# Base gathers split five and three, first pair's loads on one queue, and a third PSUM set, in a two-layer kernel

## The reference, cut to what matters

```python
c   = einsum('bsi,boi->bso', x, weight[ids])            # layer 0, adapter of the sequence
lg  = c @ W_router.T                                    # 8 experts, top 2, softmax weights w
h   = einsum('td,erd->ter', c, lora_A)
x   = x + c @ W_base.T + b_base + 2 * einsum('ter,eor,te->to', h, lora_B, w)
y   = einsum('bct,bcd->bdt', x, weights[ids])           # layer 1, over the tokens
t   = y[:, perm] in 16 heads of 64
x   = x + unpermute(gelu(t @ up) @ down)
```

## Time and profile before

| | |
|---|---|
| median of 3 runs | 623.73 us (622.9 to 623.86) |
| the profiled execution | 626.12 us |
| its span, first to last instruction | 623.7 us |
| mean granted TensorE clock | 0.991 |
| HBM read, written | 98.09 MB, 8.39 MB |

### The profile page before, as it was taken

How to read it: one execution, slowest core, us unless ns; L and a number is a source line. 1 busy time by engine, 2 the same in 40 slices (tenths; PEclk the granted TensorE clock), 3 DMA queues, 4 the chain that set the end, 5 groups by cost and what they waited for, 6 DMA issues and landing times.

```text
span 623.7 us, 13533 instructions
## 1 busy us (share of the span) xinstructions
PE 601.5 (96%) x4439; PEld 349.5 (56%) x4440; DVE 440.6 (71%) x1233; ACT 139.7 (22%) x269; POOL 127.6 (20%) x194
## 2 busy tenths in 40 slices
PE   3899999999999999999899999999999999999996
PEld 2434444444444444447667676767676767676762
DVE  3026666666666666698787997879987889887862
ACT  0310000000000000054313432314341325232333
POOL 5000000111111110042012231313131313131313
PEclk9699999999999999999999999999999999999999
DMA  8978898898999989212022222222232323222222
GB/s 272 410 265 295 293 306 288 306 302 297 311 378 404 401 296 304 71 34 62 10 60 69 92 69 87 75 80 83 66 96 64 95 62 96 64 87 67 85 60 93
DMA packets 43425, 106.89 MB, mean 171 GB/s; under 512 B 8450, under 2 KB 17666, under 8 KB 43394
## 3 DMA queue, kind: packets, MB, share of 16 engines
q1 hardware_dynamic: 30914, 76.04, 35.4%
q0 software_dynamic: 6784, 21.51, 10.4%
q10 hardware_dynamic: 5696, 8.95, 4.3%
HBM read 98.09 MB, written 8.39 MB: 171 GB/s over the span
## 4 chain that ended last, share of the span: by engine, by line
PE 92%; DVE 3%; DMA 2%; issue 1%; DVEq 0%; ACT 0%; POOL 0%; ACTq 0%; SPq 0%; POOLq 0%
PE wide L494 33%; PE bank L596 18%; PE bank L604 9%; PE bank L676 8%; PE wide L659 8%; PE y_wide L525 4%; PE wide L509 3%; PE y_wide L639 2%; DMA x_in<-x_seq_dram 2%; PE bank L617 1%; PE bank L616 1%; PE bank L620 1%; DVE c_lo L1122 1%; PE wide L474 0%; PE bank L533 0%
## 5 line engine op out<-in xcount | busy, mean ns | idle before, releaser
L494 PE MATMUL wide<-ring,x_in 128*64 128x512 f32 x960 | 208.8, 592 | 0.0
L1171 DVE STREAM_TRANSPOSE x_tok<-xres 32x128 f32<-32x128 f32 x480 | 145.1, 302 | 6.3
L1013 DVE STREAM_TRANSPOSE c_pair<-wide 32x256 f32<-32x256 f32 x240 | 107.1, 446 | 56.9 <-issue 30.1
L494 PEld LDWEIGHTS wide<-ring,x_in 128*64 128x64 f32 x960 | 68.5, 137 | 128.6 <-issue 128.6
L866 ACT ACTIVATE act_sb<-wide 128x512 f32<-128x512 f32 x120 | 66.5, 610 | 192.9 <-PE wide L659 192.9
L596 PE MATMUL bank<-c_hi,base_t 128*128 128x512 f32 x384 | 102.3, 390 | 0.0
L393 POOL DMA_INDIRECT xres<-xT_dram,row_in x32 | 35.3, 1104 | 233.1 <-DVE out_sb L1162 229.8
L596 PEld LDWEIGHTS bank<-c_hi,base_t 128*128 128x128 f32 x384 | 71.9, 188 | 15.4
L604 PE MATMUL bank<-c_lo,base_t 128*128 (+1 forms) x256 | 78.3, 391 | 0.4 <-DVE c_lo L1122 0.4
L428 POOL COPY c_all<-c_pair 128x512 f32 x30 | 19.3, 670 | 222.8 <-DVE c_pair L1013 222.8
L676 PE MATMUL bank<-act_sb,down_sb 64*64 64x512 f32 x224 | 54.3, 602 | 0.0
(11 more groups left out here) (151 smaller groups left out, 578.0 us busy)
## 6 DMA issues: line engine op xcount, KB each, us to landing
ring<-adapters_dram SPq DMA_DIRECT2D x128, 512.0 KB, 5.8
x_in<-x_seq_dram ACTq DMA_DIRECT2D x32, 256.0 KB, 4.6
up_raw<-up_dram SPq DMA_DIRECT2D x64, 64.0 KB, 2.3
down_sb<-down_dram SPq DMA_DIRECT2D x32, 128.0 KB, 2.4
ar_sb<-lora_a_router_dram ACTq DMA_DIRECT2D x1, 544.0 KB, 4.3
mix_sb<-mix_dram SPq DMA_DIRECT2D x32, 16.0 KB, 2.0
xres<-xT_dram,row_in POOLq DMA_INDIRECT x32, 3.5
out_dram<-out_sb,row_out POOLq DMA_INDIRECT x28, 2.9
```

The source lines that it names most:

```text
L494: last = pe.matmul(acc[half][h][z * TOK:(z + 1) * TOK, :], x_in[:, half, z, k, :], ring[:, k, z, h * HALF:(h + 1) * HALF], start=(k == 0), ...
L1013: last = nc.vector.transpose(c_pair[r * SQ:(r + 1) * SQ, :, q * SQ:(q + 1) * SQ], wide[half][q * SQ:(q + 1) * SQ, :, :] .rearrange("p h (k ...
L1171: last = nc.vector.transpose(x1_tok[q * SQ:(q + 1) * SQ, :].rearrange("p (c f) -> p c f", f=P)[:, :, f * SQ:(f + 1) * SQ], xres[f * SQ:(f ...
```

## The change

GpSimd issues five base gathers at first, and the other three once four blocks of pair 0 are done. TensorE turns bases 0 to 4 ahead of the twin blocks, with three sets of PSUM banks, and bases 5, 6 and 7 inside pair 1. SP now loads x of pair 0, before the ring blocks. ScalarE copies the five bases before it waits for the order, then loads x of pair 1, and copies the other three between its work for pairs 0 and 1. One value and one value load drop out of the sort, and its matmul moves to bank 0.

```diff
+SOON = 5
...
-        base_ps = [banks[4:6], banks[2:4]]
+        base_ps = [banks[4:6], banks[2:4], banks[6:8]]
+        def base_set(j):
+            return base_ps[j % 3] if j < SOON else base_ps[0]
-        sorted_ps = banks[7]
+        sorted_ps = banks[0]
...
+            def first_pair():
+                seqs = [of_order(2, 0, z, SEQS - 1) for z in range(2)]
+                first = of_order(1, 0, 0, IDS - 1)
+                for z in range(2):
+                    sp.dma_start(x_in[:, 0, z, :, :], x_seq[bass.ds(seqs[z], 1), :, :, :]
+                                 .rearrange("a p k t -> p (a k) t")).then_inc(x_in_in[0], 16)
+                for k in range(KT):
+                    sp.dma_start(ring[:, k, 0, :], adapters[bass.ds(first, 1), k * P:(k + 1) * P, :]
+                                 .rearrange("a p o -> p (a o)")).then_inc(slot_in[0][k], 16)
-            load_pair(0)
+            first_pair()
             load_pair(1)
...
-            for j in range(KT):
-                gather(base_rows[:, j, :, :].rearrange("p k o -> p (k o)"), w_base, perm_sb[:, j:j + 1], base_in[j])
+            for j in range(SOON):
+                gather_base(j)
...
+            pool.wait_ge(block_done, KT // 2)
+            on_its_own()
+            for j in range(SOON, KT):
+                gather_base(j)
             pool.wait_ge(order_ok, 1)
...
             def turn_base(j):
                 pe.wait_ge(base_in[j], 16)
-                if j >= 2:
-                    pe.wait_ge(base_turned, j - 1)
-                transposes(base_ps[j % 2], [base_rows[:, j, k, :] for k in range(KT)], base_tr)
+                if j >= 3:
+                    pe.wait_ge(base_turned, j - 2 if j < SOON else j)
+                transposes(base_set(j), [base_rows[:, j, k, :] for k in range(KT)], base_tr)
...
-            for j in range(KT // 2):
+            for j in range(SOON):
                 turn_base(j)
-            for k in range(KT // 2):
-                twin_blocks([k])
-                turn_base(KT // 2 + k)
-            twin_blocks(range(KT // 2, KT))
+            twin_blocks(range(KT))
             pe.wait_ge(loads_ok, 1)
-            pe.wait_ge(base_turned, KT)
+            pe.wait_ge(base_turned, SOON)
             pe.wait_ge(ar_in, 16)
             landed = landings(1)
-            adapter_blocks(0, 1, range(0, 5), landed)
+            adapter_blocks(0, 1, range(0, 3), landed)
+            turn_base(5)
+            adapter_blocks(0, 1, range(3, 5), landed)
             router(0)
+            turn_base(6)
             adapter_blocks(0, 1, range(5, 8), landed)
+            turn_base(7)
...
-            act.wait_ge(order_ok, 1)
-            load_x(0, 0)
-            load_x(1, 1)
-            for j in range(KT):
+            def base_copied(j):
                 act.wait_ge(base_tr, j + 1)
...
-            for t in range(2):
-                next_x(t, t)
-                tanh(t)
+            for j in range(SOON):
+                base_copied(j)
+            act.wait_ge(order_ok, 1)
+            load_x(1, 1)
+            next_x(0, 0)
+            base_copied(5)
+            base_copied(6)
+            tanh(0)
+            next_x(1, 1)
+            base_copied(7)
+            tanh(1)
...
-            sorted_by(nc.vector.tensor_scalar(cut[:, 1:2], cut[:, 0:1], -1, SEQS, ALU.mult, ALU.add))
-            back, on = (dve.value_load(cut[0:1, z:z + 1], min_val=1, max_val=SEQS - 1) for z in range(2))
+            back = dve.value_load(cut[0:1, 0:1], min_val=1, max_val=SEQS - 1)
             nc.vector.tensor_copy(order[:, 0, 0:PAIRS], lists[:, bass.ds(back + 2 * SEQS, PAIRS)])
-            sorted_by(nc.vector.tensor_copy(order[:, 0, PAIRS:SEQS], lists[:, bass.ds(on, PAIRS)]))
+            sorted_by(nc.vector.tensor_copy(order[:, 0, PAIRS:SEQS], lists[:, bass.ds(SEQS - back, PAIRS)]))
```

More of the change, by code:

```diff
@@ L133, in build @@
         equal = at(c_tok_at + 1024, "equal", [1, SEQS])
-        cut = at(c_tok_at + 1792, "cut", [1, 2], I32)
+        cut = at(c_tok_at + 1792, "cut", [1, 1], I32)
         c_pair = at(c_tok_at + 4096, "c_pair", [P, KT, P])
@@ L294, in of_order @@
                 return sp.value_load(order[0:1, row, bass.ds(t + z * PAIRS, 1)], min_val=0, max_val=most)
+            def first_pair():
[7 more added lines that the diff above has]
+                                 .rearrange("a p o -> p (a o)")).then_inc(slot_in[0][k], 16)
             def load_pair(t):
                 which = [of_order(1, t, z, IDS - 1) for z in range(2)]
-                changed = None if isinstance(t, int) and t == 0 else [of_order(3, t, z, 1) for z in range(2)]
+                changed = [of_order(3, t, z, 1) for z in range(2)]
                 def rows(z, k):
@@ L306, in rows_of @@
                     for k in range(KT):
-                        if changed is not None:
-                            sp.wait_ge(block_done, (t - 1) * KT + k + 1)
+                        sp.wait_ge(block_done, (t - 1) * KT + k + 1)
                         for z in lists:
                             rows(z, k)
-                if changed is None:
-                    rows_of((0,))
-                    return
                 if isinstance(t, int) and t == 1:
@@ L418, in _, with gather_base @@
             pool.wait_ge(perm_in, 16)
-            for j in range(KT):
+            def gather_base(j):
                 gather(base_rows[:, j, :, :].rearrange("p k o -> p (k o)"), w_base, perm_sb[:, j:j + 1], base_in[j])
+            for j in range(SOON):
+                gather_base(j)
             def keep_pair(t):
@@ L827, in _ @@
                     last = nc.scalar.copy(base_rows[:, j, h * KT // 2:(h + 1) * KT // 2, :],
-                                          base_ps[j % 2][h][:, :].rearrange("p (k o) -> p k o", o=P))
+                                          base_set(j)[h][:, :].rearrange("p (k o) -> p k o", o=P))
                 last.then_inc(base_turned, 1)
-            for t in range(2):
-                next_x(t, t)
-                tanh(t)
+            for j in range(SOON):
[9 more added lines that the diff above has]
+            tanh(1)
             with act.Fori(1, PAIRS // 2 - 1) as i:
```

## The result

| | before | after |
|---|---|---|
| median | 623.33 us (622.67 to 623.86, 5 runs) | 618.91 us (617.88 to 619.87, 5 runs) |
| the profiled execution, its span | 626.12, 623.7 | 619.76, 617.7 |
| mean granted clock in it | 0.991 | 0.995 |

The ratio is 0.9917, 95% interval 0.9897 to 0.9937: faster by 3.9 to 6.4 us, under 1%. (The two medians of the table alone would give 0.9929, a gain of 4.4.) The forecast was 616.1 us, a gain of 7.6. The sign held. The median lies outside the forecast's own range, 614.8 to 617.6, and inside the wide one, 614.8 to 619.4, which also held rival A and half of rival B.

A forecast was written before the change was run, and what follows sets the result against it. TensorE bound the kernel (busy 96%), so the first twin block's start set the end. Pair 1 starts 11.5 sooner, less 3.9 for transposes and stall: gain 7.6, 626.12 to 618.5, less 2.39: 616.1; range 614.8 to 617.6, with rivals to 619.4.

The forecast's parts named there:

- rival A: First twin block: short gaps between transposes keep the clock low, so 1.8 us of the gain stay unwon, 617.9; chance 0.17.
- rival B: Before the first block: loads behind x share SP's queue with it, start 2.6 later, clock lost, 620.5; chance 0.11.
- if the first block starts after 18: Sign of being wrong: the first twin block, forecast at 16.7, starting later than 18 us.
- The cover: Before the first block: base 4 is turned by 15.2 at full clock, 16.1 at half, ready before 16.7.
- follow at once: Early transposes: the third PSUM set lets base 2's transposes come directly after base 1's, which end at 11.6.
- 1.05 MB are in at 13.0 + 2.6 = 15.6: Before the first block: SP alone, at 0.405 MB/us behind the gathers, moves x and ring 0 by 15.6.
- the 1.1 behind it: Before the first block: a landing is told 1.1 us after its last byte, making the start 16.7.
- the 1.8 us that I counted as won: First twin block: at full clock it no longer pays the 1.8 us extra of the low clock.
- the stall of 0.4: Pair 1: late gathers share DMA with SP, so a ring block comes 0.4 us late; bounds 0 and 2.
- Three transposes: Pair 1: base transposes put between its blocks cost 1.17 us each, 3.5 in all.
- Rival C: Pair 1: late gathers lose turns to SP's backlog and hold TensorE at base 5; 625.9 if landing at 44; chance 0.03.
- Kept TensorE at 16.00 of 16.00: Pair 10, 184 to 200 us: TensorE was never idle there, so later pairs pass an earlier start on unchanged.

The follow-up runs named there:

- the repeat: The changed kernel itself, unaltered, measured once more on another set of runs: ratio to the kernel before 0.9925.
- x split: Changed kernel, with ScalarE loading the first sequence of pair 0's x ahead of its copies and SP the second: ratio to the kernel before 0.9897.
- the filler: Changed kernel plus 20 identity transposes on TensorE between base 4 and the first twin block, into an unread bank: ratio to the kernel before 0.9905.
- two sets: Changed kernel with two PSUM sets instead of three for the first five bases: ratio to the kernel before 0.9915.
- six gathers and x split: Changed kernel with six base gathers first, and x of pair 0 loaded over ScalarE's and SP's queues: ratio to the kernel before 0.9901.
- ring 0 first: Changed kernel, but SP issues ring block 0 ahead of the two x loads of pair 0: ratio to the kernel before 0.9917.
- six gathers: Changed kernel with six base gathers first and two late, base 5 turned ahead of pair 0: ratio to the kernel before 0.9906.
- x sooner: Changed kernel, but SP issues each x load of pair 0 right after its own value load, all on SP's queue: ratio to the kernel before 0.9920.

## Why the prediction was right or wrong

**The mechanism was right in the main.** Gathers held x back, five gathers first free it, and the first twin block starts sooner. Undoing the split of the gathers alone (1.0001) takes the whole gain. Three things on the way were mis-sized: the start, the low clock, and how much of a start reaches the median. Of the forecast's own signs of being wrong, "if the first block starts after 18" missed by 0.05 in one profile and came true in the repeat (18.32); the granted clock was not at 2.4 GHz in the first blocks.

**The cover was right, the order's worth unsaid.** The prediction had ScalarE's copies begin at once and so bases ready by 15.2: they were, at 15.08. That this was a condition of the gain, and worth 1.7 us (0.9954 to 0.9926; 3.1 in the profiles), stood only in that paragraph's working. The third set was listed as costing nothing and letting base 2 "follow at once"; ScalarE's early copies do that without it (11.48).

**The start: 16.7 forecast, 17.95 measured.** The step that failed is "1.05 MB are in at 13.0 + 2.6 = 15.6", with the 1.1 behind it, and both terms were too small. The first took SP's rate alone as 0.405 MB/us, read at 34 to 39 us from a queue that had been full for 15 us; behind the gathers it was 0.25 to 0.32 from 14 to 17, and 1.05 MB had moved at 16.2: 0.6 late. The second took the time from the bytes to the block from one gather; it was 1.75, and 2.4 in the repeat: 0.65 more. That the sort was over 0.5 sooner than forecast (8.47) and ring 0 was issued at 11.68 and not 12.3 gave nothing back. Why the rate dips, and why the landing stands so far behind, is open. The Trainium skill (DMA: Bandwidth & Descriptors, Issuing engines are not separate DMA queues) was weighed for rival B: it says that issuing from several engines saves only issue time. For x on ScalarE's queue or SP's the ratios agree (0.9913, 0.9917). With x split over both the first block started 1.0 sooner, in one profile; by the ratio (0.9897) a gain over the change is not shown.

**The clock: rival A came true in the profile, and the term itself was mis-sized.** I had put the fall 3.5 us behind the stop; it came 2.4 behind it (stop at 15.08, fall at 17.5). Not the short gaps between transposes that rival A names brought it, but the idle stretch: with the filler in it the clock stayed. Before the first block TensorE idled 3.3 in the repeat, 2.9 in the change, 2.6 with two sets, 2.2 with six gathers and x split, 2.1 with ring 0 first, 1.9 with x on ScalarE's queue: each time the clock was low in the first blocks, and the eight took 15.4 to 15.65. With 1.7 (x split), 1.3 (six gathers) and 1.0 (x sooner) idle, the clock stayed at 2.4 GHz. All this is from one profile each. The other half of the error is in the base of the sum. 39 more executions of the kernel before were recorded beside the experiments: 18 had a mean clock of 0.990 to 0.993 and a median span of 623.1 us, 21 had 0.997 to 1.000 and 621.8. The spans of the two kinds overlap (621.1 to 624.2, 620.7 to 623.9). The profiled execution was of the first kind. So by their mean clock more than half of the executions of before did not pay the 1.8 us that I counted as won; none of those was profiled. With 1.3 us between the kinds, 18 / 39 x 1.3 = 0.6 us were there to be won on average, 1.2 less than the 1.8. 7.6 - 1.2 is 6.4, and with the start 1.25 later 5.15, beside 5.2 by the ratio. That it meets the ratio so closely is luck: the sum leaves out the stall of 0.4 that did not come, and that the changed kernel does not keep the clock always either (0.995 twice in five executions).

**Pair 1.** Three transposes cost 3.52 as forecast. The stall of 0.4 did not come, since the start was later; with x split or sooner, at 16.97 and 17.15, it did (0.5 and, by the stretch 30 to 50 us, 0.3). The late gathers were covered: the first landed at 35.4 and was wanted at 38.5 (forecast: by 34.2, wanted at 36.0). Rival C had nothing.

**Later pairs.** "Kept TensorE at 16.00 of 16.00" is true of that execution, and the conclusion that pair 10 never waits is not: it idled 0.92 with six gathers and 0.6 with two sets. So a sooner start is not always passed on one for one.

**From the profiled execution to the median.** I subtracted 2.39 because the profiled execution of before stood that far above its median. The changed kernel's stood 0.85 above its own. By the profiles the gain is 6.4 (626.12 to 619.76): 5.15 in the changed stage, 0.85 later in the span, 0.4 outside it. Of the 0.85, 0.5 is the tail, where before waited for its last `up_raw` and the change did not. The distances of the two profiled executions from their medians differ by 1.5 (by 1.9 with the five runs of before, whose median is 623.33), and that brings 6.4 down to the 4.4 of the medians. That this too is clock and tail is argued from the 39 executions and not shown for these two.

**The range.** Its low end is 0.4 lower than its own terms: a start at 16.2 and no stall give 615.2, not 614.8. The measured 618.91 is inside only by the part added for rivals A and B.

| term | forecast | measured |
|---|---|---|
| first block | 16.7 | 17.95 |
| low clock at it | 0 | 1.5 (15.40 against 13.95, in the profile) |
| pair 1's start | 30.5 | 33.35 |
| three transposes, stall | 3.5, 0.4 | 3.52, 0 |
| gain by the profiles | 7.6 | 6.4 |
| gain by the medians | 7.6 | 4.4 (by the ratio 5.2) |

## What to carry to other kernels

Where one wait ahead of a full engine sets the end, ask what bytes stand in front of its transfer, and move what is wanted later behind it; then look at every engine that must be ready at the same time, as the gain was only whole once ScalarE's order was changed too. Do not take a queue's rate from a steady stretch for one where it has just taken over, and count the time from the bytes to the landing as a term with a spread of its own (1.1 to 2.4 us here). Before counting a low-clock stretch as won, look at the mean clock of several executions: one profile may show a loss that half of them do not have.

## What was not expected of the hardware

SP's queue alone moved 254 to 320 GB/s in the 3 us behind the gathers, 311 to 369 in another execution of the same kernel, and 414 to 426 alone, from 15 on, where another queue had been moving bytes until then (ScalarE's with x split, the sixth gather). Two executions had moved the same 1.09 MB by 16.0, and their first blocks started 1.35 us apart. Executions of one kernel fall into two kinds by their mean clock (0.991 and 0.999; median spans 1.3 us apart). And the last small load of a kernel of 618 us, 64 KB of `up_raw`, was on the path of the end in some executions, at 2.85 and 3.75 us, and not in others.
